# Order of the value matmuls and of the softmax row sums in the attention loop of a transformer layer

## What is computed

```python
lat = rmsnorm(x @ wkv_a_w.T, norm_w)
kv = lat @ wkv_b_w.T
q = (x @ wq_w.T + wq_b).reshape(B, S, H, DH)          # H = 16 heads, DH = 128
...
scores = jnp.einsum('bqhd,bkhd->bhqk', q, k) * scale
scores = jnp.where(mask, scores, -jnp.inf)            # causal
attn = jax.nn.softmax(scores, axis=-1)
o = jnp.einsum('bhqk,bkhd->bqhd', attn, v).reshape(B, S, H * DH)
return o @ out_w.T + out_b
# the layer: x = x + attn(layernorm(x)); x = x + ffn(layernorm(x))
```

## Time and profile before

| | us |
|---|---|
| median of 2 timed runs | 2605.0 (2571.2 and 2638.8) |
| the profiled execution | 2372.8 |
| span of its slowest core (core 4) | 2371.3 |
| spans of all cores | 2332.0 to 2371.3 |

### The profile page before, as it was taken

One profiled execution on the slowest core, in us unless ns is written; L12 is line 12 of the kernel. 1 busy time (PEld: TensorE's weight loads), 2 busy tenths in 40 slices (PEclk: granted clock), 3 DMA queues, 4 the chain that ended last, 5 costly groups with the idle time before them and its releaser, 6 DMA issues.

```text
span 2371.3 us, 24783 instructions; the slowest of 8 cores (2332.0 to 2371.3 us)
## 1 busy us (share of the span) xinstructions
PE 1920.5 (81%) x8635; PEld 830.2 (35%) x8797; DVE 503.9 (21%) x1069; ACT 663.0 (28%) x929; POOL 243.9 (10%) x250
## 2 busy tenths in 40 slices
PE   2498976766656766667883899999999998999998
PEld 2343433211122111112442444444444444444443
DVE  3500125444445444321114000000000000000000
ACT  5621110567702676400115211211111211000000
POOL 0001100000010000000101111111111111111110
PEclk9998878999988999857995899999999999999999
DMA  6425632000011000203994887787788778797976
GB/s 166 149 27 49 60 35 27 1 1 1 1 16 21 1 1 1 27 0 54 169 164 157 42 41 36 38 42 38 36 41 40 36 38 54 74 80 76 77 79 63
DMA packets 455050, 121.97 MB, mean 51 GB/s; under 512 B 384977, under 2 KB 450706, under 8 KB 451858
## 3 DMA queue, kind: packets, MB, share of 16 engines
q0 software_dynamic: 383872, 73.48, 44.4%
q1 hardware_dynamic: 71058, 46.90, 6.9%
HBM read 239.83 MB, written 16.78 MB: 108 GB/s over the span
## 4 chain that ended last, share of the span: by engine, by line
PE 70%; DVE 9%; DMA 8%; ACT 7%; issue 6%; DVEq 0%; ACTq 0%; SPq 0%; POOL 0%; POOLq 0%
PE PS L826 14%; PE PS L831 14%; PE PS L890 14%; PE PS L425 5%; PE PS L604 3%; PE PS L500 3%; PE PS L743 3%; DMA WT<-outwT 3%; PE PS L685 3%; DVE SQB L642 3%; PE PS L557 2%; PE PS L347 2%; PE PS L596 2%; DMA F32A<-xb 2%; ACT PB L624 2%
## 5 line engine op out<-in xcount | busy, mean ns | idle before, releaser
L826 PE MATMUL PS<-BIG,W 128*128 128x512 bf16 x1505 | 346.9, 381 | 3.7 <-DMA W<-upw 2.1
L831 PE MATMUL PS<-BIG,W 128*128 128x512 bf16 x1505 | 344.9, 379 | 1.6
L890 PE MATMUL PS<-BIG,W 128*128 128x512 bf16 x1504 | 334.0, 380 | 5.8 <-DMA W<-downw 3.1
L826 PEld LDWEIGHTS PS<-BIG,W 128*128 128x128 fp8e4 x1536 | 150.8, 98 | 184.7 <-issue 5.0
L831 PEld LDWEIGHTS PS<-BIG,W 128*128 128x128 fp8e4 x1536 | 150.3, 98 | 181.2
L890 PEld LDWEIGHTS PS<-BIG,W 128*128 128x128 fp8e4 x1536 | 150.6, 98 | 180.1 <-issue 7.4
L596 PE MATMUL PS<-SQB,ONESCb 128*1 128x512 bf16 x224 | 86.5, 386 | 114.2 <-DVE SQB L642 114.0
L624 ACT ACTIVATE X<-PS,BIASC,SCL 128x512 bf16<-128x512 f32 x224 | 156.5, 774 | 67.5 <-PE PS L616 67.2
L847 DVE TENSOR_TENSOR BIG<-PB 128x512 bf16<-128x512 bf16 x96 | 40.9, 426 | 626.8 <-ACT PB L843 626.8
L616 PE MATMUL PS<-BIG 128*128 128x512 bf16 x426 | 132.2, 389 | 27.5 <-ACT PB L624 12.8
L425 PE MATMUL PS<-BIG,WT 128*128 128x512 bf16 x500 | 135.5, 436 | 8.0 <-DMA WT<-wqT 6.9
(11 more groups left out here) (119 smaller groups left out, 1617.0 us busy)
## 6 DMA issues: line engine op xcount, KB each, us to landing
W<-gatew POOLq DMA_DIRECT2D x48, 256.0 KB, 6.4
W<-upw POOLq DMA_DIRECT2D x48, 256.0 KB, 8.3
W<-downw POOLq DMA_DIRECT2D x48, 256.0 KB, 8.1
F32A<-xb POOLq DMA_DIRECT2D x8, 1024.0 KB, 5.2
F32A<-xb SPq DMA_DIRECT2D x8, 1024.0 KB, 5.1
WT<-wqT POOLq DMA_DIRECT2D x16, 512.0 KB, 6.5
F32A<-xb SPq DMA_DIRECT2D x32, 256.0 KB, 5.8
WT<-outwT POOLq DMA_DIRECT2D x16, 512.0 KB, 9.4
```

Source lines behind the costliest of these rows:

```text
L826: mmg = kb.op("tensor", lambda e, c=c, qb=qb, bufp=bufp, pb=pb: e.matmul(PS[pb][:, :], W8[:, bufp * 2048 + c * 128:bufp * 2048 + (c + 1) * ...
L831: mmu = kb.op("tensor", lambda e, c=c, qb=qb, bufp=bufp, pb=pb: e.matmul(PS[pb + 1][:, :], W8[:, 4096 + bufp * 2048 + c * 128:4096 + bufp ...
L890: isl=(t3 == 2 and cc == 15): e.matmul(PS[pi][:, :], W8[:, slot * 2048 + cc * 128:slot * 2048 + (cc + 1) * 128], fuse_ap(c, qb), start=isf ...
```

## The change

`emit_pair` is split. `emit_avs(p)` holds the two value matmuls and waits for the exponentials of the pair's two slots, or for their masked forms (`rdy`), and not for the addition. `emit_lmm(p)` holds the ones matmul, waits for the addition and now raises sT, and its count is kept in `lmm_ct`. In step p the order on TensorE is: score matmuls of pair p, value matmuls of pair p-1, ones matmul of pair p-2. At the block's end the last value matmuls come first, then the ones matmuls of the last two pairs. The addition of pair p waits for the ones matmul of pair p-2 (before: for that pair's first value matmul, which stood behind it). Since value matmuls no longer prove that the addition has read the buffers, the exponential of slot g also waits for the addition that read slot g-8. L653 waits for the last ones matmul. The diff without its first lines (an empty `padd_ring`):

```diff
@@ -586,16 +587,13 @@
                     gstart = g_ctr[0]
                     rdy = {}
                     padd_by = {}
-
-                    def emit_pair(p, i8=i8, qb=qb, po=po, gstart=gstart, npair=None, nsl=None):
-                        kb.wait("tensor", "sV", padd_by[p])
-                        if p == 0 and pair_idx > 0:
-                            kb.wait("tensor", "sV", linv_by_pair[pair_idx - 1])
-                            if pair_idx > 1:
-                                kb.wait("tensor", "sV", otev_by_pair[pair_idx - 2])
-                        kb.op("tensor", lambda e, p=p, isf=(p == 0), isl=(p == npair - 1): e.matmul(
-                            PS[5][0:1, 0:512], ONESCb[:, 0:1], PADD[p % 2],
-                            start=isf, stop=isl))
+                    lmm_ct = {}
+
+                    def emit_avs(p, i8=i8, qb=qb, po=po, gstart=gstart, nsl=None):
+                        kb.wait("tensor", *rdy[2 * p])
+                        kb.wait("tensor", *rdy[2 * p + 1])
+                        if p == 0 and pair_idx > 1:
+                            kb.wait("tensor", "sV", otev_by_pair[pair_idx - 2])
                         for i in (2 * p, 2 * p + 1):
                             kt_i = slot_lists[qb][i]
                             pi_i = (gstart + i) % 8
@@ -606,6 +604,15 @@
                                     BIG0[:, VOFF + kt_i * 1024 + i8 * 128:VOFF + kt_i * 1024 + i8 * 128 + 128],
                                     PSL[pi_i],
                                     start=isf, stop=isl), inc="sT")
+
+                    def emit_lmm(p, npair=None):
+                        kb.wait("tensor", "sV", padd_by[p])
+                        if p == 0 and pair_idx > 0:
+                            kb.wait("tensor", "sV", linv_by_pair[pair_idx - 1])
+                        lmm_ct[p] = kb.op("tensor", lambda e, p=p, isf=(p == 0),
+                                          isl=(p == npair - 1): e.matmul(
+                            PS[5][0:1, 0:512], ONESCb[:, 0:1], PADD[p % 2],
+                            start=isf, stop=isl), inc="sT")
 
                     for j, kt in enumerate(slots):
                         g = gstart + j
@@ -621,6 +628,7 @@
                         kb.wait("scalar", "sT", t_s)
                         if g >= 8:
                             kb.wait("scalar", "sT", av_ring[g - 8])
+                            kb.wait("scalar", "sV", padd_ring[g - 8])
                         exp_ring[g] = kb.op("scalar", lambda e, pi=pi, sb_=sb_, qb=qb, kt=kt: e.activation(
                             PSL[pi], sb_[:, :], AFT.Exp,
                             bias=BIASC[:, qb * 16 + kt:qb * 16 + kt + 1],
@@ -635,19 +643,25 @@
                             rdy[j] = ("sS", exp_ring[g])
                         if j % 2 == 1:
                             p = j // 2
+                            if p >= 1:
+                                emit_avs(p - 1, nsl=nsl)
+                            if p >= 2:
+                                emit_lmm(p - 2, npair=npair)
                             kb.wait("vector", *rdy[j - 1])
                             kb.wait("vector", *rdy[j])
                             if p >= 2:
-                                kb.wait("vector", "sT", av_by[(pair_idx, 2 * (p - 2))])
+                                kb.wait("vector", "sT", lmm_ct[p - 2])
                             padd_by[p] = kb.op("vector", lambda e, p=p, gstart=gstart: e.tensor_add(
                                 PADD[p % 2], PSL[(gstart + 2 * p) % 8],
                                 PSL[(gstart + 2 * p + 1) % 8]), inc="sV")
-                            if p >= 1:
-                                emit_pair(p - 1, npair=npair, nsl=nsl)
-                    emit_pair(npair - 1, npair=npair, nsl=nsl)
+                            padd_ring[gstart + 2 * p] = padd_by[p]
+                            padd_ring[gstart + 2 * p + 1] = padd_by[p]
+                    emit_avs(npair - 1, nsl=nsl)
+                    emit_lmm(npair - 2, npair=npair)
+                    emit_lmm(npair - 1, npair=npair)
                     g_ctr[0] += nsl
                     pgl = pair_idx % 16
-                    kb.wait("vector", "sT", av_by[(pair_idx, nsl - 1)])
+                    kb.wait("vector", "sT", lmm_ct[npair - 1])
                     if (pair_idx - 1) in wr_by:
                         kb.wait("vector", *wr_by[pair_idx - 1])
                     linv_by_pair[pair_idx] = kb.op("vector", lambda e: e.tensor_copy(
```

More of the change, by code:

```diff
@@ L459, in build_nc @@
         av_by = {}
+        padd_ring = {}
         g_ctr = [0]
```

## The result

| | before | after |
|---|---|---|
| median of all timed runs, us | 2357.0 (10 runs) | 2314.9 (11 runs) |
| ratio, after to before | | 0.983, 95% interval 0.980 to 0.985 |
| profiled execution, us | 2372.8 | 2314.9 |
| span of its slowest core, us | 2371.3 | 2313.4 |

The change makes the kernel 1.7% faster, 42 us by the medians. Three of the ten timed runs of before (2571.2, 2610.7 and 2638.8, two of which stood ahead of the prediction) and three of the eleven of after (2380.6, 2514.0 and 2585.0, with a mean granted clock of 0.80 to 0.91 on the cores of one die or both, where the others have 0.93 to 0.95) are left out of the ratio as disturbed.

A forecast was written before the change was run, and what follows sets the result against it. Bound by the attention stages' latency loop through the pair addition: 3.5 us per head x 16 = 56, less 3 for low clock at stage starts, plus 1 for fewer dips, saves 54: 2605 to 2551 us, range 2310 to 2610.

The forecast's parts named there:

- What bounds the kernel: Both attention stages are latency loops through the vector engine's pair addition; no engine is full in their 226 to 235 us.
- The chain is 0.55 shorter: From an odd exponential's end to the exponential its score matmul releases: 1.36 us instead of about 1.9.
- the 0.30: Step in us from the ones matmul to the next matmul, whose weight load starts only with it; called the disputed term.
- A met wait costs nothing visible in the rows: Waits already satisfied add no time, as score matmuls with their ring wait follow at 0.22 us.
- Blocks: Lengths of the two blocks of a head: qb=1 from 15.47 to 13.4 us, qb=0 from 12.06 to 10.6.
- The end of a block: From a block's last exponential to the next block's first: 2.40 to 2.42 us, before 2.74.
- The clock: The attention stages' granted clock, 0.97 mean, may dip less with a fuller TensorE; 1 us put for it.
- The rival of a lower clock: The new loop has no slack for a low clock; two thirds of pairs low would give 2661 us; chance 0.07.
- The rival in which waits eat half: Up to three added waits per pair, up to 0.08 us each, cost 27 us: 2578; chance 0.19.
- ScalarE did not set the pace: Rival: score matmul 0.22 behind the ones matmul, ScalarE paces the loop, 23.1 us per head, 2537 in all; chance 0.12.
- The rule of the Trainium skill: Weight loads are pulled ahead of matmuls in flight; by it the 0.30 step behind the ones matmul would be 0.22.
- The level: The 54 us saving for the profiled execution (2372.8 to 2319) was carried to the timed median: 2605 to 2551.

The follow-up runs named there:

- the wait order: Changed kernel with ScalarE's wait for the addition of slot g-8 put ahead of its score matmul wait: head 24.53 us instead of 24.93, 0.978 of before.
- the 128 columns: Changed kernel with a 128 x 128 block of ones as row-sum matmul weights instead of one column: head 23.55 us, 1.38 less, 0.970 of before.

## Why the prediction came out as it did

- *What bounds the kernel*: right. The two attention stages gave the gain, and the loop through the vector engine was its cause: the pair addition no longer ends any idle time of the value matmuls.
- *The chain is 0.55 shorter*: mis-sized. It went from about 1.9 to 1.52, not to 1.36. Half of the missing 0.16 is the term taken once and present twice: I took the 0.30 over as the step behind the ones matmul, and bounded a second gap as one behind a blocked value matmul. It is the load ahead of the ones matmul itself; a change that puts other matmuls in front of it, with no idle time in between, makes it visible (0.52 from the first value matmul). The other half is the step to the exponential, nearly all of it the wait on ScalarE.
- *"A met wait costs nothing visible in the rows"*: this sentence failed too. It was read from waits in TensorE's queue. The one added wait stands on ScalarE behind the wait that comes last, at each even slot, the very ones the chain ends in. It costs 0.055 there and 0.40 per head, 6 us in all. The two waits added on TensorE cost nothing visible: the value matmuls start 0.15 after the exponential's end and 0.22 apart, as predicted.
- *Blocks*: 13.94 and 10.98 instead of 13.4 and 10.6. Taking off what the wait order gives (0.22 and 0.17) and half of what the 128 columns give (0.79 and 0.59, for two loads) leaves 13.3 and 10.5. If these effects simply add, the stepping through masked pairs was right within 0.1 us. Of the two errors, the load is the larger: 0.69 per head, 11 us in all.
- *The end of a block*: the timeline of the kernel after shows it:

```profile
488.10 1.45 ACT L632 ACTIVATE SQB<-PS,BIASC,SCL 128x512 bf16<-128x512 f32 x2 [0.18 <-PE PS L623]
...
489.69 0.59 PE L602 MATMUL PS<-SQB,BIG 128*128 128x512 bf16 x2 [0.73 <-ACT SQB L632]
...
490.21 0.59 PE L613 MATMUL PS<-SQB,ONESCb 128*1 128x512 bf16 x2
...
490.74 0.82 PE L623 MATMUL PS<-BIG 128*128 128x512 bf16 x3
...
491.28 2.79 ACT L632 ACTIVATE X<-PS,BIASC,SCL 128x512 bf16<-128x512 f32 x4 [1.73 <-PE PS L623]
```

  The last exponential starts 0.67 after 488.10, at 488.77, and the next block's first at 491.28, 2.51 us later, where the prediction had 2.42 and the kernel before has 2.74. Here the wait and the place behind the ones matmul (0.07 together) are the whole difference but 0.02. The prediction had the two ones matmuls 0.22 behind the value matmul and 0.22 to 0.30 apart; they stand 0.31 behind it and 0.22 apart, and the two errors nearly cancel.
- *The clock*: right in direction. The granted clock of the stage is 0.99 where it was 0.97, and of the 46 us by which the stages are shorter, 42 are those of 16 undisturbed heads; most of the other 4 must be the shorter time at the half clock, for which the prediction had 1 us. The rival of a lower clock did not occur. The rival in which waits eat half was right in kind and half right in size: 14 of 56 us were lost, not 27. ScalarE did not set the pace in this kernel; it does once the ones matmul is out of the chain.
- *The rule of the Trainium skill* ("TensorE: Matmul & The Clock Gate", Part 2, LDWEIGHTS) that weight loads are pulled ahead of matmuls in flight holds in these runs for loads as wide as the one before them (0.22, for 128 columns and for one) and not where a one-column and a 128-column load follow each other (0.30, in either order).
- *The level*: 2551 us was the sum made for the profiled execution (2319, measured 2315) carried over to a median of 2605. That step failed: the timed runs of after have a median of 2314.9. Seven of the ten runs of before lie between 2349 and 2358. With no row for the excess, the level of the profile was the better base. The saving itself was put at 54 us, with 43 to 66 as the forecast's own bounds, and is 42, just under them; the 2% line at 52 us that the forecast sat on was missed on the low side. That 2319 met 2315 for the profiled execution is luck: the saving was 12 us too high, and the profiled execution of before was some 16 us above the median of its timed runs, with the clock of 0.81 in the stretch of the queries.

## What to carry over

When work is taken out of a latency loop, list again every instruction and every wait that stays between the last event and the next, on each queue, also those that were hidden until then; here two gaps of 0.07 and 0.08 us took a quarter of the expected gain. Put the wait that is met last at the end of an instruction's waits. And ask first whether an instruction has to be in the loop at all: exchanging two calls took another 2.0 us off a head, after the change's own 2.6, and letting the order run across block ends 2.3 more.

## What the hardware showed

- Where a one-column weight load (0.08 us) stood behind a 128-column matmul, or a 128-column load (0.10 us) behind a one-column matmul, the load started only with its own matmul, and the matmuls started 0.30 us apart. Between two matmuls of 128 columns, and between two of one column, it was 0.22. A wider operand was faster, by 1.38 us per head.
- A wait on ScalarE whose condition was true long before still cost 0.055 us when it stood behind the wait that was met last, and nothing visible when it stood ahead of it (0.48 us from score matmul to exponential behind a value matmul, as in the kernel before without this wait).
- Exponentials of 128 x 512 follow each other at 0.67 us, below the 0.706 that the prediction worked out from the Trainium skill ("ScalarE: Activation LUTs", What ACT_TABLE_LOAD costs).
